# A four-layer graph network on one core: query copies, weight rounding, activation tables and masks moved to other places in the instruction order

## The reference

```python
xn = layernorm(x); x = x + gnn(xn, edge_index) + mix(xn)
x = x + ffn(layernorm(x))
```

## Time and profile before

| | |
|---|---|
| median of three runs | 3021.53 us (3019.8 to 3021.64) |
| the profiled execution | 3015.4 us, span 3013.6 us |
| mean granted PE clock | 0.963 |
| PE, DVE, ACT, POOL busy | 91%, 47%, 37%, 23% |
| DMA | 220.37 MB, mean 73 GB/s |

### The profile page before, as it was taken

How to read it: one execution, slowest core, us unless ns; L and a number is a source line. 1 busy time by engine, 2 the same in 40 slices (tenths; PEclk the granted TensorE clock), 3 DMA queues, 4 the chain that set the end, 5 groups by cost and what they waited for, 6 DMA issues and landing times. The chain is left out here.

```text
span 3013.6 us, 48711 instructions
## 1 busy us (share of the span) xinstructions
PE 2735.0 (91%) x20003; PEld 2488.3 (83%) x20003; DVE 1418.9 (47%) x3609; ACT 1117.7 (37%) x2085; POOL 705.8 (23%) x260
## 2 busy tenths in 40 slices
PE   8999999997669999998999899989987899997697
PEld 8999999994339878998879899988677888894597
DVE  8777565573131235478623532323735545005632
ACT  6632265551013113249322433233634234453131
POOL 0134311110002312310425143324023231112121
PEclk9999999998889999999999999999998999999799
DMA  2022221108962112220212122211001121110121
GB/s 68 12 77 74 85 69 38 54 21 315 415 278 67 48 33 64 74 85 1 71 41 74 43 77 75 80 54 59 1 17 55 52 69 59 35 32 2 32 64 58
DMA packets 163790, 220.37 MB, mean 73 GB/s; under 512 B 21521, under 2 KB 142795, under 8 KB 163570
## 3 DMA queue, kind: packets, MB, share of 16 engines
q1 hardware_dynamic: 163570, 217.26, 21.6%
HBM read 215.31 MB, written 1.92 MB: 72 GB/s over the span
## 5 line engine op out<-in xcount | busy, mean ns | idle before, releaser
L58 PE MATMUL ps<-weights_r,buf_r 128*125 128x256 f32 (+3 forms) x4080 | 548.5, 286 | 21.7 <-DVE buf_r L3238 7.6
L58 PEld LDWEIGHTS ps<-weights_r,buf_r 128*125 128x125 f32 (+1 forms) x4080 | 516.8, 188 | 25.9 <-issue 14.6
L268 POOL TENSOR_TENSOR weights_r<-weights,head_weights_r 128x1536 fp32r<-128x1536 f32 (+1 forms) x78 | 274.4, 3518 | 1121.0 <-ACT head_weights_r L261 1121.0
L268 POOL TENSOR_TENSOR weights_r<-weights,weights_r 128x1536 fp32r<-128x1536 f32 (+1 forms) x79 | 273.4, 3461 | 1036.5 <-ACT weights_r L261 1036.5
L58 PE MATMUL ps<-xT_r,weights_r 128*128 128x376 f32 (+1 forms) x2100 | 346.5, 310 | 0.0
L58 PE MATMUL ps<-head_weights_r,buf_r 128*125 128x256 f32 (+2 forms) x2400 | 329.1, 283 | 0.0
L58 PEld LDWEIGHTS ps<-xT_r,weights_r 128*128 128x128 f32 x2100 | 314.8, 189 | 4.6 <-issue 2.4
L58 PEld LDWEIGHTS ps<-head_weights_r,buf_r 128*125 128x125 f32 x2400 | 305.5, 187 | 0.0
L58 PE MATMUL ps<-weights_r,xT_r 128*125 128x256 f32 x1680 | 233.2, 283 | 7.6 <-issue 5.9
L261 ACT ACTIVATE head_weights_r<-weights 128x1536 fp32r<-128x1536 f32 (+1 forms) x78 | 114.3, 1466 | 331.8 <-PE ps L58 207.5
L58 PEld LDWEIGHTS ps<-weights_r,xT_r 128*125 128x125 f32 x1680 | 213.6, 187 | 9.6 <-issue 6.5
(11 more groups left out here) (359 smaller groups left out, 4240.0 us busy)
## 6 DMA issues: line engine op xcount, KB each, us to landing
expert_regions<-in_L_ffn_w SPq DMA_DIRECT2D x64, 576.0 KB, 15.0
expert_regions<-in_L_ffn_w SPq DMA_DIRECT2D x48, 768.0 KB, 20.5
weights<-in_L_mix_fc_w SPq DMA_DIRECT2D x24, 768.0 KB, 4.4
weights<-in_L_gnn_W SPq DMA_DIRECT2D x18, 768.0 KB, 4.6
weights<-in_L_ffn_W SPq DMA_DIRECT2D x12, 768.0 KB, 4.7
weights<-in_L_mix_w_mapT SPq DMA_DIRECT2D x9, 768.0 KB, 4.8
weights<-in_L_gnn_W_out SPq DMA_DIRECT2D x9, 768.0 KB, 4.6
weights<-in_L_mix_kqv_wT SPq DMA_DIRECT2D x9, 768.0 KB, 4.5
```

What stands on the lines that cost most here:

```text
L58: mm = net.nc.tensor.matmul(ps, net.r(stationary(s, k)), net.r(moving(m, k)), start=(n == 0 and k == 0), stop=(stop and n == 2 and k == kc ...
L268: self.nc.gpsimd.tensor_tensor(self.r(load.dst), load.dst, self.r(load.high), ALU.subtract).then_inc(self.low_made, 1)
```

## The change

- QueryApply: the two rounded copies of pair c-2 go between and behind the exponentials of pair c, four exponentials ahead of each. The copies of the last two pairs come at the end. DVE's and PE's orders stay.
- SoftmaxPairs: the two roundings of weights go into the last pair's order, one behind the spreads and one behind the first "hi". The barrier's mark for the high buffers is the last transpose of the last pair on PE instead of the ends of the stage on all engines. POOL's part stays.
- A one-element ACTIVATE without a semaphore, `load_table`, stands at the start of the ACT part of LinearNorm, LinearResidualNorm, LinearReluNorm (Sqrt), SoftmaxPairs, TokenSoftmax, TopTwo (Exp), SlotFirst (Gelu), and behind the root in Degrees (Exp).
- The self loops and masks of layer 0 go from before KvSummary to behind PhiSquares, before the output projection.

```diff
@@ Net
-    def barrier(self, stage):
-
-        self.high_used = [used + stage.ends() for used in self.high_used]
+    def barrier(self, stage, marks):
+
+        self.high_used = [used + marks for used in self.high_used]
...
+    def load_table(self, func):
+
+        self.nc.scalar.activation(self.table[:1, :], self.lnc[:1, 0:1], func, scale=0.0)
@@ QueryApply.__init__
         for c in range(self.PAIRS + 1):
             if c <= last:
                 pe += [("phi", c, *q) for q in self.pieces]
-                act += [("phi", c, *q) for q in self.pieces]
+                act += [("phi", c, *q) for q in self.pieces[:4]]
+            act += [("high", c - 2, 0)] if c > 1 else []
+            if c <= last:
+                act += [("phi", c, *q) for q in self.pieces[4:]]
+            act += [("high", c - 2, 1)] if c > 1 else []
             if c > 0:
                 pe += [(kind, c - 1, j) for j in range(2) for kind in ("den", "out")]
-                act += [("high", c - 1, j) for j in range(2)]
...
+        act += [("high", last, j) for j in range(2)]
         dve.append(("low", last, 1))
@@ LinearNorm, LinearResidualNorm and LinearReluNorm.scalar (TokenSoftmax, TopTwo and SoftmaxPairs: Exp; SlotFirst: Gelu)
     def scalar(self, act):
+        self.net.load_table(ACT.Sqrt)
         self.begin(act)
@@ Heads
-            net.barrier(self)
+            net.barrier(self, self.high_free())
...
+    def high_free(self):
+
+        return self.ends()
@@ SoftmaxPairs.step, for the last pair
-            act += [("spread", c, 0), ("spread", c, 1), ("hi", c, 0), ("hi", c, 1)]
+            act += [("spread", c, 0), ("spread", c, 1), ("weights", c, 0), ("hi", c, 0), ("weights", c, 1), ("hi", c, 1)]
@@ SoftmaxPairs
+    def high_free(self):
+
+        last = self.v.shape[2] // 128 - 1
+        return [(self.net.pe.sem, self.at["pe"]["turn", last, 1, NT - 1, 1])]
@@ SoftmaxPairs.scalar
         for q in self.order["act"]:
             c = q[1]
+            if q[0] == "weights":
+                self.net.split_high(self.next_unit + q[2], self.next_segment)
+                continue
...
-        self.split_next(self.net.split_high)
@@ Degrees.scalar
         self.nc.scalar.activation(self.rdeg, self.rdeg, ACT.Sqrt).then_inc(self.net.act.sem, self.net.act.one())
+        self.net.load_table(ACT.Exp)
@@ network, layer 0
     linear_T(net, XT, w, feat(G[0]), cols=(0, D), evac="a", after=start)
-    loops = SelfLoops(net, ALU.add, unpack.ends())
     bias_out = AddRow(net, R, net.row(ins["L0_mix_b_out"]), now() + head_norm.ends())
...
     squares = PhiSquares(net, phi, phi_squares)
+    loops = SelfLoops(net, ALU.add, unpack.ends())
     linear(net, pair(G[2], G[1]), ins["L0_mix_w_outT"], R, "add", add=R, after=now() + bias_out.ends(), tiles=turned.made)
```

More of the change, by code:

```diff
@@ L149, in __init__ @@
         self.mv = self.st[:TP, 60:70].rearrange("p (t s) -> p t s", t=NT)
+        self.table = sb("table_scratch", [128, 1])
         self.ones, self.zeros, self.iota64 = sb("ones", [128, 128]), sb("zeros", [128, HALF]), sb("iota64", [128, 64])
@@ L1773, in schedule @@
         bases = dict(pe=net.pe.planned, act=net.act.planned, dve=net.dve.planned, pool=net.pool.planned)
-        self.at = {e: {q: bases[e] + i + 1 for i, q in enumerate(seq)} for e, seq in self.order.items()}
+        counted = {e: [q for q in seq if q[0] != "weights"] for e, seq in self.order.items()}
+        self.at = {e: {q: bases[e] + i + 1 for i, q in enumerate(seq)} for e, seq in counted.items()}
         if first >= 0:
@@ L1781, in schedule @@
             net.freed[b] = ({"act": net.act, "dve": net.dve}[engine].sem, self.at[engine][entry])
-        self.take(**{e: len(seq) for e, seq in self.order.items()})
+        self.take(**{e: len(seq) for e, seq in counted.items()})
         if n_heads > 1 and not last:
-            net.barrier(self)
+            net.barrier(self, self.high_free())
     def banks(self):
         return {q: self.net.bank() for q in self.order["pe"]}
+    def high_free(self):
+        return self.ends()
     def ps(self, q, p, w):
@@ L2782, in scalar @@
     def scalar(self, act):
+        self.net.load_table(ACT.Gelu)
         self.begin(act)
@@ L2804, in __init__ @@
             s.last.used, s.last.used_at = [(net.pe.sem, self.turn_done(self.TURNS - 1))], (len(net.stages) - 1, 1 << 20)
-        net.barrier(self)
+        net.barrier(self, self.ends())
     def sync(self, sp):
```

## The result

The changed kernel takes 2984.69 us (median of four runs, 2980.74 to 2985.41), the kernel before 3021.59 (3019.8 to 3025.36). The ratio is 0.9876 with a 95% interval of 0.9861 to 0.9891: 37 us less, where 34.5 were forecast. The profiled executions took 2980.74 and 3015.4 us, 34.7 apart. Each is shorter than the median of its kernel, and the executions of one kernel differ by 3 to 15 us, so what two traces show need not meet the difference of the medians to the microsecond.

The account below looks back on a forecast made before the run. PE (TensorE), busy 2735.0 of 3013.6 us, was taken as the bound. Savings of 14.4 + 7.2 + 7.9 + 5.1 = 34.6 us off the 3021.5 us median gave 2986.9, range 2984 to 2992.

Parts of the forecast that it names:

- Query copies: QueryApply: copies between the exponentials bring four pair periods from 49.13 to 34.8 us, saving 14.4, some 3 of it clock.
- Weights: Softmax tail: rounding inside the last pair starts PE 5.7 us earlier, and 1.5 us of low clock behind goes; sum 7.2.
- Masks: Wait for key summaries: moving the masks saves 5.5 of 6.4 us, plus 2.4 by the clock; sum 7.9.
- Tables: Token softmax, first scores, norm after the small MLP, last router: loads run ahead save 1.28 us each, 5.1 in all.
- Places costed at nothing: The other seven table-load places give nothing; layer 1's Sqrt and the Gelu between expert passes 0, up to 1.28 us.
- The clock isn't given back: Rival: low-clock stretches come anyway, so 27.3 us saved, total 2994; chance 0.17.
- Another chain binds: Rival: query loop bound by ACT behind DVE or PE's banks, its part 0 to 5 us, total 2997 to 3001; chance 0.10.
- A dearer switch: Rival: the engine drains at table switches, four exposed places give a second 1.28 us each, total 2982; chance 0.03.
- Loads repeated: Rival: another function restores the old table, four exposed loads stay, more loads than now, total 2992; chance 0.04.
- The clock falls: Rival: PE's granted clock falls in the whole run; at 0.951 the gain is gone, at 0.945 3038 us; chance 0.04.

Follow-up runs that it names:

- the part alone: The kernel before with the moved query copies alone: 3004.8 us, ratio 0.9949.
- the filled pause: The kernel before with 50 identity products on PE between the key summaries and the wait for them, masks unmoved: 3020.73 us, ratio 1.0015.

## Why the prediction was right, step by step

- **Query copies, 14.4 forecast.** The trace has 14.0 (periods of 8.78, not 8.69), the part alone 15.4 by the runs. The bound I named, PE's own products, is the bound. The reason I gave for the copies being free, that their input is one period old, was wrong; it is 0.9 and 3.8 us old from the start of the period. The number survived because the edit puts each behind enough exponentials; the prediction had timed only the reader of the copies, DVE's subtraction, not their input, so here it was lucky. Taken at its word my reason would have called the old order free as well, and that order costs 17 us. The clock's share was there too: 1.00 in the loop instead of 0.92.
- **Weights, 5.7 + 1.5.** 6.52 - 0.59 = 5.93, and the window at 1.00 instead of 0.81. PE started at the time that low(5, 0), held by POOL, allowed, as forecast; the second one was held too (2.98 us) at no cost. The Trainium skill ("GPSIMD Engine Reference", Specifications) says that the two engines share their SBUF interfaces; these rows agree.
- **Masks, 5.5 + 2.4.** 6.4 - 0.77 = 5.6, the window at 1.00 instead of 0.74, the masks at 2.06 us, no wait for a bank.
- **Tables, 4 x 1.28 (about 3.2 arrived).** DVE's wait across the first use fell from 2.33 to 1.06 us at the token softmax, from 2.00 to 0.44 at the norm, from 1.50 to 0.22 at the last router, and ACT's first exponential of the scores starts 0.12 us after its input instead of 1.40. Not all of that reached PE. At the first scores PE gains 1.5 us and at the last router 1.3. At the norm its wait fell from 3.42 to 1.85 us, but the 42 products ahead of it ran longer at the lower clock (0.74 in the 12.4 us from 2251.9, where the 12.5 us from 2269.1 of before had 0.82), and from them to the first product of the next stage (2299.18 before, 2281.48 after) it is 29.6 us instead of 30.1: 0.4 us less. In the kernel with the tables alone the same products ran at 1.00. PE's rows of before, of after and of that kernel:

```profile
2269.12 9.14 PE L58 MATMUL ps<-weights_r,buf_r 96*125 96x384 f32 x42 [2.88 <-DVE buf L3043]
```

```profile
2251.86 10.58 PE L58 MATMUL ps<-weights_r,buf_r 96*125 96x384 f32 x42 [2.88 <-DVE buf L3071]
```

```profile
2269.73 7.61 PE L58 MATMUL ps<-weights_r,buf_r 96*125 96x384 f32 x42 [2.88 <-DVE buf L3063]
```

  The step that failed is the first: the token softmax was counted as exposed because a chain waits behind it, but that chain ends in the stream of expert weights, whose DMA share of 1.02 I had used to cost the Gelu load at nothing and not this one. 1.3 us too much there and 0.9 at the norm, hidden by the rest.
- **Places costed at nothing.** In front of layer 1 the load didn't run ahead: it landed behind the second rounding at 880.29, which waits for its DMA, and the root came at 881.70 for an input of 880.61. The scaling was then held by POOL until 884.58, so it cost nothing, as forecast.
- **The rivals.** "The clock isn't given back" is refuted in three windows and by the filled pause. "Another chain binds" by the periods. "A dearer switch" by 1.39 us. "Loads repeated" by their number. "The clock falls" by 0.967. The total of 37 against 34.5 lies within the interval (33 to 42). Set product by product against before, PE gains in the two traces 8.0 us at the masks, 7.3 at the weights, 14.9 in and behind the query loop, 1.5 at the scores, 0.9 within 65 us around the norm and 1.5 around the last router, 34.1 in all. The rest nets to 0.6, and of it pieces as large as 1.6 us stand on both sides at places that no edit touches. So the larger parts are right at their places, and that the two traces differ by the forecast to 0.1 us is luck.

## What to carry to other kernels

An instruction that waits in an in-order queue costs what stands behind it; write down, for each of its inputs, how far into the period it is made, and put it directly behind the last other work that ends by then. A table loaded ahead pays only where nothing behind it waits anyway: read the idle time behind the load as well as the one before it. A shorter wait is not yet a gain: compare where PE's products before and behind the place start, as the norm shows. Removing one pause of PE gives back more than the pause where the trace shows a lower clock behind it, here 1.4 to 2.4 us for 6 us.

## What the runs showed of the hardware that I had not expected

**The same work takes 546.5 or 552.2 us, by the time at which it starts.** From the first router of layer 1 to the norm ahead of the MLP (1155.09 to 1701.69 in the trace of before) no kernel here changes a wait of PE. Where it started at 1146.9 us or from 1152.9 to 1156.8 it lasted 546.4 to 546.6 us, in ten executions; started at 1149.5 and 1150.9 it lasted 552.2, at 1151.3 and 1151.4 549.6. PE's idle time in it is the same (33.8 to 33.9 us); the products run at the lower clock behind some of PE's pauses in one case and not in the other. The whole stretch in the kernel with the masks alone, and in before (columns as above): the same 3992 products keep PE busy for 518.3 and for 512.8 us.

```profile
1149.50:1701.70 552.20, 518.29 (x3992) 490.14 (x3992) 306.73 (x876) 226.49 (x404) 156.31 (x56) 0.99 0.18 56
```

```profile
1155.10:1701.70 546.60, 512.75 (x3992) 486.42 (x3992) 306.46 (x876) 225.97 (x403) 156.15 (x56) 1.00 0.19 57
```

The stretch around the norm (2265 to 2330 of before) is another: in the kernel with the weights alone, where no load there moved, PE gains 3.2 us in it by the clock, in the change 0.9, load included. The pause of 0.68 us at 2672.95 is a third. In the nine executions with the tables loaded ahead the 8 us behind it ran at 1.00, in the five others at 0.79, which is 1.5 us, though no load was moved near it.

So an edit early in the program can move all that follows into or out of such places, at a price (up to 5.7 us here) that has nothing to do with what it edits. It explains most of why the masks alone gained 8.0 us at their place and nothing in the profiled execution: 5.6 were lost here, and 1.5 and 0.9 more in the same way around 300 and 1710 us. How much of the spread of the runs it makes (6 to 11 us between runs of the kernel before in one group) isn't shown, since most kernels were traced once. A gain under 5 us is better read from the starts of PE's products on both sides of its place than from the total. That the start time decides is what the fourteen traces fit, with nothing tried that sets it; what fixes these places stays open.

**A DVE instruction was held through several instructions of POOL, or through one.** A subtraction of 0.55 us lasted 6.24 us (2711.47 to 2717.71, the change run again) beside this one of POOL's merged rows:

```profile
2708.38 8.92 POOL L1467 TENSOR_TENSOR resid<-resid,row 125x768 f32<-125x768 f32 x5
```

```profile
2711.47 6.24 DVE L729 TENSOR_TENSOR buf_r<-buf,xT_r 128x375 fp32r<-128x375 f32 x1
```

POOL's row is five instructions of some 1.8 us each. Four of them end while the subtraction lasts, the last at 2717.30, and DVE is through 0.41 us behind it. In the first profile of the change the same subtraction lasted 0.92 us, though POOL's row ran from 2701.31 to 2710.55 around it: it ended 0.40 us behind one of the five (2704.91), and POOL's next took 2.14 us instead of 1.83. In the softmax tail each hold lasted to the end of one POOL instruction. So the hold ends behind the end of some POOL instruction, which one depends on how the two meet, and its size was not to be foreseen from the rows of before.
